# Differential attention with top-2 routed experts on one core: the difference of the one-tile chunk is made by VectorE in every second pair of heads only, by GpSimd in the others

## The chip, the cores and the metric

The kernel runs on one core of one Trainium2 chip. The metric is the device time of one execution in microseconds (us); less is better. The engines are TensorE (PE, with its weight loads as PEld), VectorE (DVE), ScalarE (ACT), GpSimd (POOL) and SyncE (SP, which issues the DMAs of the hardware queue).

## The reference: what is computed

`x` is 8 sequences of 512 tokens of 128 features. One layer of attention with 16 heads of 8 features and two key projections, then a layer of 8 experts of which each token takes 2:

```
s1 = q @ k1.T * SCALE ; s2 = q @ k2.T * SCALE          (causal mask on both)
attn = softmax(s1) - sigmoid(lambda) * softmax(s2)
attn = attn / max(sum(abs(attn)), 1e-6)
x  = layernorm(x + (attn @ v) @ Wo.T)
xn = layernorm(x) * gamma + beta ; p = softmax(xn @ router.T / 1.5)
x  = layernorm(x + sum over the top 2 experts e of p[e] * silu(xn @ W1[e]) @ W2[e])
```

## The kernel before

**Chunks and slots.** One body of the program handles one sequence ("batch") `b`. The attention of a batch is cut into 40 chunks, one for each slot of a body: 8 pairs of heads with 5 chunks each (`SLOTS = PAIRS * KINDS`). A chunk is a row of 512 score columns. The kind of a chunk (`c % 5`) says which query tiles of the pair it holds: kind 0 is one tile of 512 columns (tile 3 of the first head), kind 3 the same of the second head, kind 2 two tiles of 256 columns, kinds 1 and 4 one of 384 and one of 128. Chunks 0, 10, 20, 30 are of kind 0 in the even pairs, chunks 5, 15, 25, 35 of kind 0 in the odd pairs.

**What a chunk goes through.** PE writes both score maps to PSUM (lines 1117, 1119; slot `c`). DVE takes the row maxima (line 989, same slot). ACT makes `exp` with the row sums (line 700, slot `c+1`), into the ring `exps` with 7 places. DVE inverts the second sum (`inv_l2`, line 964, slot `c+2`); POOL makes `lam_l1` from the first (line 614). Then comes the difference `exps2 * coefficient - exps1`, written over the second half of the same ring place (`diff = exps[:, :, 1, :]`, so that the profile names it `exps`). POOL makes it at slot `c+4` with one TENSOR_SCALAR for each tile (line 623) and one TENSOR_TENSOR of 512 columns (line 627). For the kinds in `DVE_KINDS = (0,)` DVE makes it at slot `c+3` in place of POOL: a `coef` of one column (line 974) and one fused SCALAR_TENSOR_TENSOR of 512 columns (line 978). DVE sums the absolute values (line 999, slot `c+5`), PE transposes the difference (line 1151, slot `c+5`), ACT copies it out (line 707), PE multiplies with the values (line 1140).

**Side tasks.** The work of everything else is laid in between by hand, in tables that give each task its slot. Prep tasks (`PREP_SLOTS`) make the projections of batch `b+1`; POOL's part of them is lines 635 and 637, SP's part comes `PARTS_SLOT` slots later. Post tasks belong to batch `b-1` for slots 0 to 39, to `b-2` for 40 to 79, to `b-3` from 80 on: `count` (slot 29) and `place` (31) work out where each token goes; `scatter` (8 indirect DMAs issued by POOL, line 646) writes the tokens to DRAM in the order of the experts; `sorted` (43) loads them back as `xg` (SP, line 498); `turn` (44, 51, 58, 65) transposes four tiles on PE (line 1086); `hidden` and `expert` are the two matmuls of each of 15 tiles (lines 1094 and 1100; DVE's part of `hidden` is `hT`, line 934); `y_out` stores four tiles (SP, line 516); `gather` (8 indirect DMAs on POOL, line 655) fetches them back and `combine` adds them (DVE, line 946). DVE does its part of a task one slot after the table's slot, POOL two slots after, PE, ACT and SP in it. Within a slot every engine runs its queue in the order of the program: chunk work and side tasks have no priority over one another.

**Banks.** The PSUM results of side tasks go in turn to two banks, `side0` and `side1` (`placed_in % banks`, in order of the tasks). A task waits until the reader of the task before it in the same bank is done (line 1034).

**The semaphores of the difference.** `diff_ready(n, c)` gives the semaphore and the count on which ACT (ring place free), DVE (line 996) and PE (line 1148) wait: `diff_dve_done` for a chunk made by DVE, `diff_done` for one made by POOL.

Of the kernel before, what the change touches and what calls it, by code (L numbers as in the profile page):

```python
# [61 lines left out]
EXP_RING, DIFF_RING = 7, 12  # L62


DVE_KINDS = (0,)
PAIR_CHUNKS = (((3, 0, 0),), ((2, 0, 0), (0, 0, 384)), ((1, 0, 0), (1, 1, 256)), ((3, 1, 0),), ((2, 1, 0), (0, 1, 384)))
PLACE_OF_TILE = {3: 0, 2: 1, 0: 2, 1: 3}
PAIRS = NH // 2
KINDS = len(PAIR_CHUNKS)
SLOTS = PAIRS * KINDS  # L70
# [12 lines left out]

SIDE = {}
POST_SLOTS = {"spread": 7, "den_T": 10, "divide": 10, "out_proj": 12, "norms": 17, "xn_T": 21, "logits": 23, "router_exp": 24, "count": 29, "place": 31, "sorted": 43, "norm3": 96, "finish": 98}
HIDDEN_SLOTS = (45, 46, 49, 51, 53, 55, 59, 60, 64, 66, 68, 70, 73, 75, 77)
EXPERT_SLOTS = (48, 50, 52, 54, 56, 58, 62, 63, 67, 69, 71, 73, 76, 77, 79)
WEIGHT_SLOTS = (41, 43, 45, 47, 49, 51, 55, 56, 61, 62, 62, 66, 69, 70, 70)
TURN_SLOTS = (44, 51, 58, 65)
Y_OUT_SLOTS = (57, 67, 77, 83)  # L90
SCATTER_SLOTS = (31, 32, 32, 34, 34, 35, 36, 37)
GATHER_SLOTS = (82, 83, 85, 85, 87, 88, 88, 90)
COMBINE_SLOTS = (86, 86, 88, 90, 91, 91, 91, 93)
STACK_SLOT = 33
WEIGHTS_AHEAD = 4
PARTS_SLOT = 7
PREP_SLOTS = (15, 18, 22, 23, 24)


def units_of(c):  # L100

    pair, kind = divmod(c, KINDS)
    first = pair * 2 * NT
    for t, second, col in PAIR_CHUNKS[kind]:
        yield t, pair, second, col, first + NT * second + PLACE_OF_TILE[t]
# [15 lines left out]

REDUCTIONS = [0]
EXPS = [0]
SCALED = [0]
for _c in range(SLOTS):
    REDUCTIONS.append(REDUCTIONS[-1] + len(reductions(_c)))
    EXPS.append(EXPS[-1] + 2 * len(list(units_of(_c))))
    SCALED.append(SCALED[-1] + (0 if _c % KINDS in DVE_KINDS else len(list(units_of(_c)))))
SETS = PAIRS * len(SUM_SETS)


# [63 lines left out]
def build(nc, x, wqT, wk1T, wk2T, wvT, woT, lam, gamma, beta, rwT, w12, out):  # L195
    ctx = ExitStack()
    with ctx:  # L197
# [8 lines left out]
        def signal(name, per_batch, step=1):  # L206
            signals.append(Signal(ctx.enter_context(nc.semaphore(name)), per_batch, step))
            return signals[-1]
# [118 lines left out]
        inv_l2_done = signal("inv_l2_done", SETS)  # L327
        lam_l1_done = signal("lam_l1_done", SETS)
        scaled_done = signal("scaled_done", SCALED[SLOTS])
        diff_done = signal("diff_done", PAIRS * (KINDS - len(DVE_KINDS)))  # L330
        coef_done = signal("coef_done", PAIRS * len(DVE_KINDS))
        diff_dve_done = signal("diff_dve_done", PAIRS * len(DVE_KINDS))
        abs_done = signal("abs_done", REDUCTIONS[SLOTS])
        trans_done = signal("trans_done", SLOTS)
        diffT_copied = signal("diffT_copied", SLOTS)
# [114 lines left out]

        def diff_ready(n, c):

            pair, kind = divmod(c, KINDS)
            here = kind in DVE_KINDS
            same = [i for i in range(KINDS) if (i in DVE_KINDS) == here]
            made, count = (diff_dve_done if here else diff_done), pair * len(same) + sum(i <= kind for i in same)
            return made.sem, made.after(n, count)

        def earlier(n, c, by):
# [109 lines left out]
        def _(pool):  # L569
# [29 lines left out]
            def body(b, stages):  # L599
                for slot in range(SLOTS):  # L600
                    for n, c in chunks(b, stages, slot, LAG_DIFF):
                        pair, kind = divmod(c, KINDS)
                        ring = ring_e(n, c)
                        count = pair * len(SUM_SETS) + SUM_SET_OF[kind] + 1
                        if kind in (0, 2, 3):
# [7 lines left out]
                                lam_all[:, head_of(pair, kind // 3):head_of(pair, kind // 3) + 1].broadcast_to([P, wide])  # L613
                            nc.gpsimd.tensor_tensor(lam_l1[:, mine], sums[:, 0, mine], lam, ALU.mult)\
                                .then_inc(lam_l1_done.sem, 1)
                        if kind in DVE_KINDS:
                            continue

                        pool.wait_ge(lam_l1_done.sem, lam_l1_done.after(n, count))
# [9 lines left out]
                    for task, n, bank in side_tasks(b, slot, 2 * LAG_SIDE):  # L629
# [9 lines left out]
                        if name == "scatter":  # L639
                            i = task[2]  # L640
# [8 lines left out]
                        if name == "gather":  # L649
                            i = task[2]  # L650
# [116 lines left out]
        def _(dve):  # L767
# [69 lines left out]
            def body(b, stages):  # L837
                for slot in range(SLOTS):
                    route(b, stages, slot, 0)
                    for n, c in chunks(b, stages, slot, LAG_DEN):  # L840
                        if (c + 1) % (SLOTS // 2) == 0:

                            i = (c + 1) // (SLOTS // 2)
# [5 lines left out]
                    for task, n, bank in side_tasks(b, slot, LAG_SIDE):  # L849
# [77 lines left out]
                        if name == "hidden":  # L927
                            j = task[2]
                            i = n * TILES + j
# [7 lines left out]
                        if name == "combine":  # L937
                            i = task[2]
# [25 lines left out]
                            nc.vector.reciprocal(inv_l2[:, mine], sums[:, 1, mine]).then_inc(inv_l2_done.sem, 1)  # L964
                    for n, c in chunks(b, stages, slot, LAG_EXP + 2):
                        pair, kind = divmod(c, KINDS)
                        if kind in DVE_KINDS:

                            (t, _, second, _, i), ring = next(units_of(c)), ring_e(n, c)
                            h = head_of(pair, second)  # L970
                            count = pair * len(DVE_KINDS) + DVE_KINDS.index(kind) + 1
                            dve.wait_ge(exp_done.sem, exp_done.after(n, EXPS[c + 1]))
                            dve.wait_ge(inv_l2_done.sem, inv_l2_done.after(n, pair * len(SUM_SETS) + SUM_SET_OF[kind] + 1))
                            nc.vector.tensor_scalar(coef[:, i:i + 1], sums[:, 0, i:i + 1], lam_all[:, h:h + 1],
                                                    inv_l2[:, i:i + 1], ALU.mult, ALU.mult)\
                                .then_inc(coef_done.sem, 1)
                            dve.wait_ge(coef_done.sem, coef_done.after(n, count))
                            nc.vector.scalar_tensor_tensor(out=diff[:, ring, :], in0=exps[:, ring, 1, :],
                                                           scalar=coef[:, i:i + 1], in1=exps[:, ring, 0, :],
                                                           op0=ALU.mult, op1=ALU.subtract).then_inc(diff_dve_done.sem, 1)  # L980
# [200 lines left out]
```

## Time and profile before

| what | value |
|---|---|
| median of 3 runs | 1152.73 us (1149.02 to 1153.8) |
| the profiled execution | 1139.17 us, span 1137.3 us |
| DVE busy | 935.6 us, 82% of the span |
| PE busy / PEld busy | 908.5 us, 80% / 726.7 us, 64% |
| POOL busy | 846.0 us, 74% |
| ACT busy | 841.1 us, 74% |
| mean granted clock of PE | 0.877 |

The shares are means over the whole span. The span has a start of some 60 us, in which the first batch has no neighbours, seven bodies in which attention and side tasks run together, and an end from about 1017 us on, in which only side tasks of the last batch are left. The execution that was profiled was 13.6 us faster than the median of the runs beside it, so durations are set against its own 1139.17 us.

### The profile page before, as it was taken

What the parts mean: (1) busy time and instruction counts of PE and PEld (TensorE: products, weight loads), DVE (VectorE), ACT (ScalarE), POOL (GpSimd) and SP (SyncE); (2) the same over time, 40 slices, a digit from 0 to 9 for tenths busy, and PEclk for the clock granted to TensorE, in tenths of its full rate; (3) what the DMA queues carried; (4) which work ended last, traced back from release to release, by engine and by line L of the source; (5) the groups of instructions that cost most, each with busy time, mean ns of one, the idle gap of its engine ahead of it and who ended that gap; (6) DMA issues with size and microseconds to landing.
All of it is one profiled execution on the core that took longest, in us unless ns stands there. A gap on an engine that the chain in (4) does not pass through costs nothing. (4 is left out here: it accounts for less than half of the span.)

```text
span 1137.3 us, 27887 instructions
## 1 busy us (share of the span) xinstructions
PE 908.5 (80%) x8522; PEld 726.7 (64%) x8522; DVE 935.6 (82%) x2425; ACT 841.1 (74%) x2706; POOL 846.0 (74%) x1144
## 2 busy tenths in 40 slices
PE   2487877879889788978889778978889888978681
PEld 1255555657678576766677566767677676768571
DVE  0499998889998899899999899889999899955132
ACT  1499988688887788788888788787888778853130
POOL 3389978788778888698778988798878986781503
PEclk9579788778998899889999899889999799988696
DMA  3703400533246623482237523582237523246562
GB/s 100 177 10 98 108 1 16 140 100 117 84 122 176 182 76 108 132 246 88 75 122 186 174 74 108 156 238 71 77 120 198 154 73 113 87 147 198 172 215 61
DMA packets 117045, 139.38 MB, mean 123 GB/s; under 512 B 11042, under 2 KB 99490, under 8 KB 116898
## 3 DMA queue, kind: packets, MB, share of 16 engines
q1 hardware_dynamic: 112802, 129.21, 38.3%
q0 software_dynamic: 4096, 8.40, 2.6%
q8 instruction: 69, 1.13, 0.4%
q14 instruction: 78, 0.64, 0.2%
HBM read 107.81 MB, written 29.75 MB: 121 GB/s over the span
## 5 line engine op out<-in xcount | busy, mean ns | idle before, releaser
L700 ACT ACTIVATE exps<-scores,neg_max 128x512 f32<-128x512 f32 (+3 forms) x1024 | 542.9, 551 | 102.1 <-DVE neg_max L989 101.1
L989 DVE TENSOR_REDUCE neg_max<-scores 128x1 f32<-128x512 f32 (+3 forms) x896 | 423.4, 524 | 51.3 <-PE scores L1119 49.1
L627 POOL TENSOR_TENSOR exps<-exps 128x512 f32<-128x512 f32 x256 | 326.7, 1276 | 21.4
L623 POOL TENSOR_SCALAR exps<-exps,inv_l,lam_l 128x384 f32<-128x384 f32 (+3 forms) x448 | 272.7, 615 | 87.2 <-DVE inv_l L964 75.6
L1151 PE MATMUL trans<-ident,exps 128*128 128x128 f32 x1280 | 234.6, 313 | 91.3 <-ACT diffT L707 69.3
L1117 PE MATMUL scores<-stack 72*128 72x512 bf16 (+3 forms) x1024 | 272.6, 335 | 16.6 <-DMA stack<-parts_dram 15.6
L1151 PEld LDWEIGHTS trans<-ident,exps 128*128 128x128 f32 x1280 | 158.4, 158 | 155.3 <-issue 95.3
L700 ACT ACTIVATION_READ_ACCUMULATOR exps<-scores,neg_max 128x1 f32 x1024 | 235.8, 230 | 0.0
L999 DVE TENSOR_REDUCE abs_sum<-exps 128x1 f32<-128x512 f32 (+3 forms) x448 | 222.8, 520 | 8.8 <-POOL exps L627 8.8
L707 ACT ACTIVATE diffT<-trans 128x512 f32<-128x512 f32 x320 | 196.4, 614 | 35.1 <-PE trans L1151 34.3
L1119 PE MATMUL scores<-causal_bf,ident_bf 128*128 128x128 bf16 x1024 | 209.0, 237 | 0.0
L1117 PEld LDWEIGHTS scores<-stack 72*128 72x128 bf16 x1024 | 110.6, 108 | 68.5 <-DMA stack<-parts_dram 15.8
L1094 PE MATMUL side<-xgT,w_sb 128*128 128x128 f32 x792 | 121.3, 301 | 1.9 <-DMA w_sb<-w_dram 1.0
L1100 PE MATMUL side<-w_sb,hT 128*128 128x128 f32 x824 | 114.6, 283 | 6.4 <-DVE hT L934 6.4
L1119 PEld LDWEIGHTS scores<-causal_bf,ident_bf 128*128 128x128 bf16 x1024 | 111.2, 109 | 6.9
L1094 PEld LDWEIGHTS side<-xgT,w_sb 128*128 128x128 f32 x792 | 107.5, 211 | 11.8 <-issue 4.8
L1100 PEld LDWEIGHTS side<-w_sb,hT 128*128 128x128 f32 x824 | 102.2, 195 | 10.6 <-DVE hT L934 6.7
L1140 PE MATMUL heads<-diffT,v_sb 128*32 128x128 f32 x2560 | 106.8, 287 | 0.0
L646 POOL DMA_INDIRECT x_sorted_dram<-xh,place_int x64 | 66.8, 1043 | 44.7 <-DVE owner_int L925 29.9
L655 POOL DMA_INDIRECT y_back<-y_sorted_dram,place_int x64 | 63.7, 995 | 46.0 <-issue 44.4
L1140 PEld LDWEIGHTS heads<-diffT,v_sb 128*32 128x32 f32 x2560 | 62.2, 112 | 29.1 <-issue 16.6
L753 ACT ACTIVATE tanh_sb<-side 128x512 f32<-128x512 f32 x99 | 60.6, 613 | 25.8 <-PE side L1094 25.1
(138 smaller groups left out, 921.6 us busy)
## 6 DMA issues: line engine op xcount, KB each, us to landing
w_sb<-w_dram SPq DMA_DIRECT2D x120, 512.0 KB, 3.8
stack<-parts_dram SPq DMA_DIRECT2D x288, 96.0 KB
parts_dram<-parts SPq DMA_DIRECT2D x104, 128.0 KB
xg<-x_sorted_dram SPq DMA_DIRECT2D x24, 256.0 KB, 4.2
y_sorted_dram<-y_sorted SPq DMA_DIRECT2D x24, 256.0 KB, 4.5
x_in<-x_dram SPq DMA_DIRECT2D x8, 256.0 KB, 4.7
x_res<-x_dram SPq DMA_DIRECT2D x8, 256.0 KB, 4.8
o_dram<-y_out SPq DMA_DIRECT2D x8, 256.0 KB, 2.3
```

Source lines behind the costliest of these rows:

```text
L623: nc.gpsimd.tensor_scalar(diff[:, ring, col:col + w], exps[:, ring, 1, col:col + w], inv_l2[:, i:i + 1], lam_l1[:, i:i + 1], ALU.mult, ALU ...
L627: nc.gpsimd.tensor_tensor(diff[:, ring, :], diff[:, ring, :], exps[:, ring, 0, :], ALU.subtract)\
L700: nc.scalar.activation(exps[:, ring, k, col:col + w], scores[:, c % 2, k, col:col + w], ACT.Exp, bias=neg_max[:, c % 2, k, i:i + 1], accum ...
L707: nc.scalar.activation(diffT[:, ring_d(n, c), :], trans[:, :], ACT.Copy)\
L989: nc.vector.tensor_reduce(neg_max[:, c % 2, k, i:i + many], scores[:, c % 2, k, col:col + many * w].rearrange("p (i w) -> p i w", w=w), AX ...
L999: nc.vector.tensor_reduce(abs_sum[:, place:place + (many - 1) * step + 1:step], diff[:, ring_e(n, c), col:col + many * w].rearrange("p (i ...
L1094: last = nc.tensor.matmul(bank[:, f * P:(f + 1) * P], w12_sb[:, w, f * P:(f + 1) * P], xgT[:, j // NT % 2, j % NT, :], start=True, stop=True)
L1100: last = nc.tensor.matmul(bank[:, 0:D], hT[:, (n * TILES + j) % 2, f, :], w12_sb[:, (n * TILES + j) % WEIGHTS_AHEAD, F + f * D:F + (f + 1) ...
L1117: nc.tensor.matmul(scores[:, c % 2, k, col:col + w], stack[:, 0, h, t * P:(t + 1) * P], stack[:, 1 + k, h, 0:w], start=True, stop=False)
L1119: last = nc.tensor.matmul(scores[:, c % 2, k, col + w - P:col + w], ident_bf[:, :], causal_bf[:, :], start=False, stop=True)
L1140: last = nc.tensor.matmul(heads[k * STRIP:(k + 1) * STRIP, t * P:(t + 1) * P], v_sb[:, i, NG * k + g, :], diffT[:, ring_d(n, source), col: ...
L1151: last = nc.tensor.transpose(trans[:, i * P:(i + 1) * P], diff[:, ring_e(n, c), i * P:(i + 1) * P], ident[:, :])
```

## The change

`DVE_KINDS` goes. In its place `DVE_CHUNKS` lists the chunks whose difference DVE makes: 5, 15, 25 and 35, one in each odd pair. The difference of chunks 0, 10, 20 and 30 is made by POOL, as those of the kinds 1 to 4 are. The counts of the semaphores follow. Beside it the tables of the side tasks differ: `hidden` and `expert` of tiles 9 to 14 come two slots later (of the 15 `hidden` tasks the last now has slot 79, of the `expert` tasks 81), the weights of tiles 2 to 14 one to three slots later, one `y_out`, one `scatter` a slot later, one projection a slot earlier, and SP's store of the parts a slot earlier.

```diff
-DVE_KINDS = (0,)
...
-HIDDEN_SLOTS = (45, 46, 49, 51, 53, 55, 59, 60, 64, 66, 68, 70, 73, 75, 77)
-EXPERT_SLOTS = (48, 50, 52, 54, 56, 58, 62, 63, 67, 69, 71, 73, 76, 77, 79)
+HIDDEN_SLOTS = (45, 46, 49, 51, 53, 55, 59, 60, 64, 68, 70, 72, 75, 77, 79)
+EXPERT_SLOTS = (48, 50, 52, 54, 56, 58, 62, 63, 67, 71, 73, 75, 78, 79, 81)
...
-SCATTER_SLOTS = (31, 32, 32, 34, 34, 35, 36, 37)
+SCATTER_SLOTS = (31, 32, 33, 34, 34, 35, 36, 37)
...
+DVE_CHUNKS = [c for c in range(SLOTS) if c % (2 * KINDS) == KINDS]
 SCALED = [0]
 for _c in range(SLOTS):
...
-    SCALED.append(SCALED[-1] + (0 if _c % KINDS in DVE_KINDS else len(list(units_of(_c)))))
+    SCALED.append(SCALED[-1] + (0 if _c in DVE_CHUNKS else len(list(units_of(_c)))))
...
-            pair, kind = divmod(c, KINDS)
-            here = kind in DVE_KINDS
-            same = [i for i in range(KINDS) if (i in DVE_KINDS) == here]
-            made, count = (diff_dve_done if here else diff_done), pair * len(same) + sum(i <= kind for i in same)
+            by_dve = sum(i <= c for i in DVE_CHUNKS)
+            made, count = (diff_dve_done, by_dve) if c in DVE_CHUNKS else (diff_done, c + 1 - by_dve)
             return made.sem, made.after(n, count)
...
-                        if kind in DVE_KINDS:
+                        if c in DVE_CHUNKS:
                             continue
...
-                        if kind in DVE_KINDS:
+                        if c in DVE_CHUNKS:
...
-                            count = pair * len(DVE_KINDS) + DVE_KINDS.index(kind) + 1
+                            count = DVE_CHUNKS.index(c) + 1
```

POOL's queue at slots 33 to 35, from the first scatter of a batch on, before (line 646 is the scatter, 614 `lam_l1`, 623 and 627 the difference):

```order
L646 DMA x_sorted_dram<-xh,place_int 1920x128
L614 TENSOR_TENSOR lam_l<-sums,lam_all 128x3
L646 DMA x_sorted_dram<-xh,place_int 1920x128 x2
L623 TENSOR_SCALAR exps<-exps,inv_l,lam_l 128x384
L623 TENSOR_SCALAR exps<-exps,inv_l,lam_l 128x128
L627 TENSOR_TENSOR exps<-exps 128x512
```

And after (the program is two lines shorter above this place, so 644 is the scatter, 612 `lam_l1`, 621 and 625 the difference):

```order
L644 DMA x_sorted_dram<-xh,place_int 1920x128
L612 TENSOR_TENSOR lam_l<-sums,lam_all 128x3
L621 TENSOR_SCALAR exps<-exps,inv_l,lam_l 128x512
L625 TENSOR_TENSOR exps<-exps 128x512
L644 DMA x_sorted_dram<-xh,place_int 1920x128
L621 TENSOR_SCALAR exps<-exps,inv_l,lam_l 128x384
L621 TENSOR_SCALAR exps<-exps,inv_l,lam_l 128x128
L625 TENSOR_TENSOR exps<-exps 128x512
L644 DMA x_sorted_dram<-xh,place_int 1920x128
```

The two instructions of chunk 30 stand between the first scatter and the second, and the third scatter stands behind chunk 31.

PE's queue at slots 28 and 29 of a batch in the middle, around `count`, before (line 1094 is `hidden`, 1100 `expert`, 1069 `count`; the matmuls of the scores are left out):

```order
L1094 MATMUL side0<-xgT,w12_sb 128x128 x4
L1140 MATMUL heads<-diffT,v_sb 32x128 x4
L1151 MATMUL trans<-ident,exps 128x128 x4
...
L1100 MATMUL side1<-w12_sb,hT 128x128 x4
L1069 MATMUL side0<-ones,hit 8x1 x4
```

And after (1092 is `hidden`, 1098 `expert`, 1067 `count`), from slot 27 on:

```order
L1098 MATMUL side0<-w12_sb,hT 128x128 x4
L1138 MATMUL heads<-diffT,v_sb 32x128 x8
L1149 MATMUL trans<-ident,exps 128x128 x4
...
L1092 MATMUL side1<-xgT,w12_sb 128x128 x4
L1138 MATMUL heads<-diffT,v_sb 32x128 x4
L1149 MATMUL trans<-ident,exps 128x128 x4
...
L1067 MATMUL side0<-ones,hit 8x1 x4
```

Before, `count` writes the bank of the `hidden` task of the slot ahead of it, which DVE reads; after, it writes the bank of an `expert` task two slots back, which ACT reads.

## Rows read from the trace of the kernel before

**Rows 1.** Windows: length; busy PE, PEld, DVE, ACT, POOL; clock; DMA. Two batches.

```profile
62.50:158.50 96.00, 76.92 (x754) 53.75 (x754) 92.36 (x224) 89.38 (x302) 85.36 (x119) 0.86 0.23 62
...
526.60:652.40 125.80, 105.95 (x1065) 85.48 (x1065) 118.26 (x303) 104.09 (x339) 105.56 (x140) 0.95 0.45 136
```

**Rows 2.** Waits from 183.1 to 906.7 us: us in total, times, longest.

```profile
DVE neg_max L989 <- PE scores L1119: 30.0, 29, 4.4
...
DVE abs_sum L999 <- POOL exps L627: 1.3, 4, 0.4
...
POOL exps L623 <- DVE inv_l L964: 55.9, 46, 2.4
```

**Rows 3.** Windows of three stretches: first batch, slots 13 to 32, 33 to 44.

```profile
79.00:137.00 58.00, 47.08 (x455) 32.60 (x452) 55.65 (x133) 55.73 (x188) 54.74 (x76) 0.88 0.34 90
541.00:602.00 61.00, 52.94 (x538) 43.01 (x536) 57.58 (x159) 49.51 (x159) 47.87 (x66) 0.97 0.30 97
602.00:639.00 37.00, 31.32 (x302) 24.00 (x300) 33.13 (x79) 32.01 (x107) 32.89 (x43) 0.86 0.87 248
```

**Rows 4.** Timeline of DVE, slot 13: start us, us, what.

```profile
541.30 0.14 DVE L964 RECIPROCAL inv_l<-sums 128x3 f32<-128x3 f32 x1
541.55 0.27 DVE L974 TENSOR_SCALAR coef<-sums,lam_all,inv_l 128x1 f32<-128x1 f32 x1
...
542.53 1.28 DVE L989 TENSOR_REDUCE neg_max<-scores 128x1 f32<-128x512 f32 x2
```

**Rows 5.** DVE's fused difference: all 64 (ns min/median/max), and one at slot 3.

```profile
L978 DVE SCALAR_TENSOR_TENSOR exps<-exps,coef x64: 750/958/1817, 48.9 to 995.9; 128x512 f32<-128x512 f32 x64
...
503.99 1.70 DVE L978 SCALAR_TENSOR_TENSOR exps<-exps,coef 128x512 f32<-128x512 f32 x1
```

**Rows 6.** Groups by form, DVE: busy, mean ns | idle before.

```profile
L934 DVE SCALAR_TENSOR_TENSOR hT<-tanh_sb,side 128x512 f32<-128x512 f32 x99 | 67.0, 677 | 11.5 <-ACT tanh_sb L753 11.3
```

**Rows 7.** Timeline of POOL around the scatters of one batch.

```profile
470.59 0.77 POOL L623 TENSOR_SCALAR exps<-exps,inv_l,lam_l 128x512 f32<-128x512 f32 x1 [2.44 <-DVE inv_l L964]
471.44 1.27 POOL L627 TENSOR_TENSOR exps<-exps 128x512 f32<-128x512 f32 x1
...
476.85 1.11 POOL L646 DMA_INDIRECT x_sorted_dram<-xh,place_int  x1 [1.72 <-DVE owner_int L925]
...
496.60 0.98 POOL L646 DMA_INDIRECT x_sorted_dram<-xh,place_int  x1 [0.17 <-issue]
...
505.12 1.52 POOL L623 TENSOR_SCALAR exps<-exps,inv_l,lam_l 128x384 f32<-128x384 f32 x2
...
509.43 1.09 POOL L623 TENSOR_SCALAR exps<-exps,inv_l,lam_l 128x384 f32<-128x384 f32 x2
...
517.20 0.77 POOL L623 TENSOR_SCALAR exps<-exps,inv_l,lam_l 128x512 f32<-128x512 f32 x1 [1.24 <-DVE inv_l L964]
```

**Rows 8.** Timelines of SP, PE and DVE, the chain from the scatters on.

```profile
500.48 0.44 SPq L516 DMA_DIRECT2D y_sorted_dram<-y_sorted  x1
501.34 4.35 SPq L498 DMA_DIRECT2D xg<-x_sorted_dram  x4
...
509.56 1.09 PE L1086 MATMUL side<-ident,xg 128*128 128x128 f32 x4 [1.97 <-DMA xg<-x_sorted_dram]
...
513.35 1.29 DVE L989 TENSOR_REDUCE neg_max<-scores 128x1 f32<-128x512 f32 x2 [3.22 <-PE scores L1119]
...
532.03 0.60 PE L1086 MATMUL side<-ident,xg 128*128 128x128 f32 x4
```

**Rows 9.** PE at `count`, DVE at `place`, and windows with PE's granted clock.

```profile
464.70 0.35 PE L1069 MATMUL side<-ones,hit 128*8 128x1 f32 x8 [2.22 <-DVE hT L934]
...
474.95 0.22 DVE L906 TENSOR_TENSOR place_of<-hit,side 128x64 f32<-128x64 f32 x1 [2.31 <-PE side L1080]
...
464.30:474.30 10.00, 9.60 (x65) 8.55 (x65) 7.61 (x20) 6.15 (x21) 6.09 (x9) 0.66 0.22 64
...
504.30:514.30 10.00, 7.84 (x47) 5.26 (x46) 6.75 (x14) 6.31 (x20) 9.35 (x13) 0.50 0.85 267
```

More of the change, by code:

```diff
@@ L85 @@
 POST_SLOTS = {"spread": 7, "den_T": 10, "divide": 10, "out_proj": 12, "norms": 17, "xn_T": 21, "logits": 23, "router_exp": 24, "count": 29, "place": 31, "sorted": 43, "norm3": 96, "finish": 98}
-HIDDEN_SLOTS = (45, 46, 49, 51, 53, 55, 59, 60, 64, 66, 68, 70, 73, 75, 77)
-EXPERT_SLOTS = (48, 50, 52, 54, 56, 58, 62, 63, 67, 69, 71, 73, 76, 77, 79)
-WEIGHT_SLOTS = (41, 43, 45, 47, 49, 51, 55, 56, 61, 62, 62, 66, 69, 70, 70)
+HIDDEN_SLOTS = (45, 46, 49, 51, 53, 55, 59, 60, 64, 68, 70, 72, 75, 77, 79)
+EXPERT_SLOTS = (48, 50, 52, 54, 56, 58, 62, 63, 67, 71, 73, 75, 78, 79, 81)
+WEIGHT_SLOTS = (41, 43, 46, 48, 50, 52, 56, 57, 62, 65, 65, 69, 72, 73, 73)
 TURN_SLOTS = (44, 51, 58, 65)
-Y_OUT_SLOTS = (57, 67, 77, 83)
-SCATTER_SLOTS = (31, 32, 32, 34, 34, 35, 36, 37)
+Y_OUT_SLOTS = (57, 68, 77, 83)
+SCATTER_SLOTS = (31, 32, 33, 34, 34, 35, 36, 37)
 GATHER_SLOTS = (82, 83, 85, 85, 87, 88, 88, 90)
@@ L95 @@
 WEIGHTS_AHEAD = 4
-PARTS_SLOT = 7
-PREP_SLOTS = (15, 18, 22, 23, 24)
+PARTS_SLOT = 6
+PREP_SLOTS = (15, 18, 21, 23, 24)
 def units_of(c):
@@ L329, in build @@
         scaled_done = signal("scaled_done", SCALED[SLOTS])
-        diff_done = signal("diff_done", PAIRS * (KINDS - len(DVE_KINDS)))
-        coef_done = signal("coef_done", PAIRS * len(DVE_KINDS))
-        diff_dve_done = signal("diff_dve_done", PAIRS * len(DVE_KINDS))
+        diff_done = signal("diff_done", SLOTS - len(DVE_CHUNKS))
+        coef_done = signal("coef_done", len(DVE_CHUNKS))
+        diff_dve_done = signal("diff_dve_done", len(DVE_CHUNKS))
         abs_done = signal("abs_done", REDUCTIONS[SLOTS])
```

## The prediction

> **What bounds the kernel now.** I read the windows first, one batch at a time, because the shares of the whole span mix stages. A batch with experts takes 125.8 us; DVE is busy for 118.3 of them and POOL for 105.6 [rows 1]. Then I read the waits of the six middle batches: in 724 us DVE waits 30.0 us for scores and only 1.3 us for POOL, while POOL waits 55.9 us for DVE's reciprocal [rows 2]. So DVE is mostly the engine that sets the pace, and POOL follows with slack. But the slack isn't spread evenly. In slots 13 to 32 DVE is busy for 57.6 of 61.0 us and POOL for 47.9; in slots 33 to 44 it is 33.1 and 32.9 of 37.0 [rows 3]. The timeline of POOL shows why. Its last wait is 1.72 us in front of the first scatter, at 476.85; from there it works without a wait for data until 517.20, where it waits 1.24 us [rows 7]. Inside that run lies a chain that everything follows: last scatter at 496.60, SP's load of `xg` at 501.34, PE's transposes at 509.56 after 1.97 us of waiting for that load, and DVE's next maxima at 513.35 after 3.22 us without work [rows 7, 8]. The reader is to see two regimes in each body: a long one that DVE sets (A, from slot 5 to `place`) and a short one that POOL's queue sets (B, from `place` to slot 44).
>
> **What the change costs and saves.** Durations come from the profiled execution, so the sum starts at its 1139.17 us; the median of the runs shown is 1152.73, 1.2% above, and I scale the result by that.
>
> One chunk taken from DVE: with the pair, the reciprocal starts at 541.30, `coef` at 541.55, and the next maxima start at 542.53 [rows 4]. Without it the maxima would follow the reciprocal's 0.14 us at about 541.4. That is 1.1 us. The dearest case is at slot 3, where the fused operation alone took 1.70 us in place of 0.75 [rows 5], so about 2 us. Four chunks a batch, 32 in all.
>
> One chunk given to POOL: TENSOR_SCALAR of 512 columns 0.77 us, TENSOR_TENSOR 1.27 us, and the 0.08 us between them [rows 7]: 2.1 us, 67 us in all. It is nearly twice what DVE is spared, so the change pays only where POOL's part falls on idle time.
>
> The Trainium skill (GPSIMD Engine Reference, Key points and Engine selection) says that GpSimd is about half as fast as VectorE on a two-input operation, and that it contends with VectorE instructions that read two SBUF tensors. The first speaks against this change and the rows agree (1.27 us for POOL's half of the work). By the second, taking away 32 such DVE instructions would also speed POOL up: its two TENSOR_SCALARs took 1.52 us beside a DVE pair and 1.09 us without one [rows 7], which would be 32 x 0.43 = 13.8 us of POOL's time back. The rows bear that out only for chunk 0, since at slot 13 the pair ran at its floor [rows 4, 5]; I leave it out of the sum.
>
> *Regime A.* Chunks 10 and 20 leave DVE: 2 x 1.1. In the six bodies that carry expert work, one `hT` of 0.68 us [rows 6] also moves from before `place` to behind it (DVE runs `hidden` one slot late: 12 tasks up to slot 72 before, 11 after). POOL gets 4.2 us more in a stretch where it is idle for 13 of 61 us [rows 3], which hides it; uncovered it would cost 4.2 us a body. A gives 7 x 2.2 + 6 x 0.7 = 19.6 us back.
>
> *Regime B.* Chunk 30 goes into POOL's queue between the first and the second scatter. Behind it wait seven scatters, and for them SP's `xg` load, PE's `turn` and all of DVE behind that. DVE is spared chunks 30 and 0 here and gets the moved `hT`, but it was not the one waited for. Each of seven bodies pays 2.1 us: 14.7 us. Chunk 0 comes behind the last scatter, in front of the first gather; the 1.24 us wait at 517.20 and the next ones absorb it, so I count nothing. If that cover is gone it is 2.1 us a body.
>
> *First batch.* From 79 to 137 us there are no experts, DVE is busy for 55.7 and POOL for 54.7 of 58.0 us [rows 3]. Two chunks (20 and 30) add 4.2 us to POOL; it can give back at most 58.0 - 54.7 = 3.3 us of gaps. So it costs 1 to 4 us; I take 4, as those gaps are between instructions.
>
> *The bank of `count`.* PE stood still 2.22 us in front of `count`, waiting for DVE's read of a `hidden` result [rows 9]. In the new order the bank was last an `expert` result that ACT has read. Behind that stall PE's granted clock is 0.66 in the mean of 464.3 to 474.3, so at 1.2 GHz for part of it, and DVE then waits 2.31 us for `place` [rows 9]. A PE that is not stalled may stay at 2.4 GHz and finish `place` sooner. The bound is 0 on one side and POOL's own wait of 1.72 us there on the other [rows 7]; I take 1.0 us in each of six bodies: 6 us gained.
>
> *Clock at slot 44.* From 504.3 to 514.3 the clock was 0.50 [rows 9], and the first `turn` took 1.09 us where the next took 0.60 [rows 8]. PE had no side matmuls in slots 40 to 43; now it has one `hidden` at 39 and the last `expert` at 41. Three such groups lie on the chain (transposes, values, transposes), some 1.4 us. Between nothing and all of it I take 0.7 in five bodies: 3.5 us gained.
>
> *The end.* Tile 9's `hidden` now comes behind tile 8's `expert`, one place where PE no longer has work while it waits: 1 us lost. Weights, `y_out` and the prep slots move by about as much as the work that uses them, and no engine waits long for them: 0.
>
> Sum: 1139.2 - 19.6 + 14.7 + 4 - 6 - 3.5 + 1 = 1129.8 us; times 1152.73 / 1139.17 that is **1143 us**.
>
> **The rivals.**
>
> 1. *The trade cancels.* The clock falls as before in both places. Then the sum is 1139.2 - 19.6 + 14.7 + 4 + 1 = 1139.3, or 1153 us. For it: POOL sets more of the time from `place` to slot 44 now, and PE waits on POOL there. Against it: the stall at `count` is really gone.
> 2. *GpSimd's queue stays behind (the slower side).* Chunk 0 in front of the gathers isn't absorbed: POOL goes from 476.85 to 517.20 with 4.2 us more and only 1.24 us of waiting to give, then has the gathers. If it is still late when PE wants the next difference, each of seven bodies pays 2.1 us more and the clock gains nothing: 1139.3 + 14.7 = 1154.0, or 1168 us. It decides once POOL has no wait left between `place` and slot 14. Against it: PE and DVE stand 1.97 and 3.22 us for `xg` in just that stretch [rows 8], in which POOL catches up.
> 3. *DVE is the bound everywhere and POOL's queue is elastic.* All 32 chunks at 1.1 us, the `hT` moves change nothing: 35 us less, 1104, or 1117 us. For it: DVE's 118.3 of 125.8 us. Against it: the chain over the scatters, in which the added work stands in line.
> 4. *The last tile comes too late.* `expert` 14 moves to slot 81 and its store, which waits for it, stays at 83, in front of `xg` on SP's queue. Before, that store was issued at 500.48 and `xg` at 501.34 [rows 8]; about one slot of 3.1 us (125.8 / 40) is the price if it slips past the scatters' end: 6 x 3.1 on the cancelled sum, 1158, or 1172 us. Against it: the scatters now end 2.1 us later too.
>
> **How the numbers follow.** Chances: forecast 0.42 (own range 1136 to 1150), rival 1 0.27, rival 2 0.16, rival 3 0.07, rival 4 0.08. The range of 8 in 10 has to reach into rivals 2 and 3, since both signs hold much of the chance: 1128 to 1164. A measurement of this kernel can tell about 0.5% from no change: below 1147 is faster, above 1158.5 slower. Faster: 0.33 of the forecast, 0.05 of rival 1, all of rival 3, so 0.45. Slower: 0.14 of rival 2, 0.05 of rival 4, 0.05 of rival 1 and 0.01 of the forecast, 0.25. Within: 0.30.
>
> **What would show it.** In the profile after: DVE's line 978 (by its new number) 32 times, POOL's TENSOR_SCALAR of 512 columns 96 times; DVE busy about 900 us, POOL about 911. POOL's wait for the reciprocal falls from 55.9 to some 25 us in the six middle batches. From the first to the last scatter 21.9 us in place of 19.8. No wait of PE for `hT` in front of `count`, and a shorter wait of DVE in front of `place`. The first batch some 100 us in place of 96.0. The prediction is wrong if POOL's queue isn't what `xg` waits for, if `place` isn't sooner with the stall gone, or if the waits of DVE on POOL's differences (1.3 us) grow to tens of us.

## The result: 3.3% slower, and the profile after

| | before | after |
|---|---|---|
| median | 1150.88 us (1148.64 to 1153.8) | **1187.51 us** (1184.9 to 1191.45) |
| ratio | | 1.0331, 95% interval 1.0295 to 1.0366 |

The forecast was 1143 us, faster; the time is 37 us slower and outside the range. The profiled execution of the changed kernel took 1184.9 us (span 1183.1); that of the kernel before was itself 12 us under its median, so the two traces set side by side overstate the difference by some 9 us (45.7 against 36.6). Later runs went to chips of different speed (the kernel before took 1153.26 us on the chip of `e1` to `e4` and 1136.5 on those of the others), so each is given as a ratio to the kernel before on its own chip. Traces of `e3` and `e0` are from different chips. Line numbers of the kernels with the other split are 2 lower than those of before.

The page of the changed kernel, the busy times and the groups that answer to [rows 2, 5, 6] (busy, mean ns | idle before, by whom):

```profile
PE 919.1 (78%) x8522; PEld 731.2 (62%) x8522; DVE 924.7 (78%) x2361; ACT 841.4 (71%) x2706; POOL 900.3 (76%) x1208
...
L625 POOL TENSOR_TENSOR exps<-exps 128x512 f32<-128x512 f32 x288 | 367.1, 1275 | 24.0
...
L1149 PEld LDWEIGHTS trans<-ident,exps 128*128 128x128 f32 x1280 | 157.2, 156 | 185.9 <-POOL exps L625 93.9
L997 DVE TENSOR_REDUCE abs_sum<-exps 128x1 f32<-128x512 f32 (+3 forms) x448 | 223.7, 522 | 24.6 <-POOL exps L625 24.4
```

POOL rose by 54 us and DVE fell by only 11. No engine is busier than 78%: the kernel lost time by waiting. Whole windows, the first batch and two bodies (columns as in [rows 1]):

```profile
61.70:159.30 97.60, 76.25 (x756) 53.04 (x754) 89.95 (x217) 88.67 (x302) 91.79 (x128) 0.87 0.26 61
401.30:534.80 133.50, 108.29 (x1065) 86.86 (x1065) 118.78 (x295) 104.69 (x339) 114.76 (x151) 0.94 0.44 129
534.80:663.60 128.80, 112.13 (x1065) 90.77 (x1065) 115.31 (x295) 104.42 (x339) 109.13 (x145) 0.89 0.46 132
```

The first batch took 97.6 us where it had taken 96.0, and the bodies 119 to 134 where the one of [rows 1] took 125.8. The last copy of the last chunk comes 29 us later than in the trace of before, and the stretch behind it, in which only side tasks are left, is 17 us longer (141 us for 124). Little can be read from that last part: its program is the same in `e0` and `e3`, and it took 124 us in one and 136 in the other. Who waited, from slot 8 of the second batch to slot 8 of the eighth (184 to 928.7 us; total, times, longest):

```profile
DVE neg_max L987 <- PE scores L1117: 38.6, 43, 5.2
DVE abs_sum L997 <- POOL exps L625: 13.9, 20, 2.1
...
DVE rest L855 <- ACT parts L717: 9.1, 6, 1.8
...
PE trans L1149 <- POOL exps L625: 36.9, 29, 2.8
...
PE side L1067 <- DVE hit L829: 11.9, 6, 2.1
...
POOL exps L621 <- DVE inv_l L962: 44.3, 37, 2.5
```

DVE now waits 13.9 us for POOL where it waited 1.3 [rows 2], and PE waits 36.9 us for POOL's differences where it waited 13.1 (21.0 in `e0`, another execution of the same kernel). But POOL itself still waits 44.3 us for DVE: each is late for the other at different places, and neither is simply the bound.

### The profile page after: what moved, and what is told of

Read it like the earlier page. It is cut to its first block and busy times, and to the rows that moved or that the text cites. A ratio compares the mean times of both kernels' runs of the same rounds, so it can differ in the third digit from the quotient of the medians.

```text
span 1183.1 us, 27887 instructions
## 1 busy us (share of the span) xinstructions
PE 919.1 (78%) x8522; PEld 731.2 (62%) x8522; DVE 924.7 (78%) x2361; ACT 841.4 (71%) x2706; POOL 900.3 (76%) x1208
## 5 line engine op out<-in xcount | busy, mean ns | idle before, releaser
L625 POOL TENSOR_TENSOR exps<-exps 128x512 f32<-128x512 f32 x288 | 367.1, 1275 | 24.0
L621 POOL TENSOR_SCALAR exps<-exps,inv_l,lam_l 128x384 f32<-128x384 f32 (+3 forms) x480 | 292.5, 615 | 72.2 <-DVE inv_l L962 55.9
L997 DVE TENSOR_REDUCE abs_sum<-exps 128x1 f32<-128x512 f32 (+3 forms) x448 | 223.7, 522 | 24.6 <-POOL exps L625 24.4
L1098 PE MATMUL side<-w_sb,hT 128*128 128x128 f32 x808 | 116.6, 290 | 11.1 <-DVE hT L932 10.9
L1138 PE MATMUL heads<-diffT,v_sb 128*32 128x128 f32 x2560 | 110.6, 288 | 3.9 <-issue 3.8
L644 POOL DMA_INDIRECT x_sorted_dram<-xh,place_int x64 | 67.3, 1052 | 42.4 <-DVE owner_int L923 31.4
L932 DVE SCALAR_TENSOR_TENSOR hT<-tanh_sb,side 128x512 f32<-128x512 f32 x100 | 67.6, 676 | 26.2 <-ACT tanh_sb L751 24.9
```

What stands on the lines that cost most here:

```text
L621: nc.gpsimd.tensor_scalar(diff[:, ring, col:col + w], exps[:, ring, 1, col:col + w], inv_l2[:, i:i + 1], lam_l1[:, i:i + 1], ALU.mult, ALU ...
L625: nc.gpsimd.tensor_tensor(diff[:, ring, :], diff[:, ring, :], exps[:, ring, 0, :], ALU.subtract)\
L997: nc.vector.tensor_reduce(abs_sum[:, place:place + (many - 1) * step + 1:step], diff[:, ring_e(n, c), col:col + many * w].rearrange("p (i ...
L1098: last = nc.tensor.matmul(bank[:, 0:D], hT[:, (n * TILES + j) % 2, f, :], w12_sb[:, (n * TILES + j) % WEIGHTS_AHEAD, F + f * D:F + (f + 1) ...
L1138: last = nc.tensor.matmul(heads[k * STRIP:(k + 1) * STRIP, t * P:(t + 1) * P], v_sb[:, i, NG * k + g, :], diffT[:, ring_d(n, source), col: ...
```

## The experiments

**Which part costs: the split or the tables?** The change holds two things. Each was run alone, and then the parts of each. `e1` is the changed kernel with all tables of before; `e2` the kernel before with all new tables.

> Only the split of the difference is changed (GpSimd makes chunks 0, 10, 20, 30); every table of side tasks is that of before. Theory Q (GpSimd's queue): the seven bodies of the changed kernel are 22.6 us longer because GpSimd has 2.1 us more per chunk where it has no slack, and the 23.2 us after the last of them come from the tables; this kernel then takes about 1151 + 22 = 1173 us. Theory T (tables): all of the loss comes from the later expert tasks; this kernel then takes 1151 us or a little less.

> Only the tables are changed; VectorE makes the difference of every chunk of kind 0, as before. Theory Q: 1151 + 23 = 1174 us, nearly all of the difference after 928 us. Theory T: 1187 us.

Measured 1172.76 us, 1.0198 (1.0150 to 1.0246), for the split and 1172.20 us, 1.0191 (1.0138 to 1.0243), for the tables. Two almost equal losses, whose product 1.039 is near the 1.033 of both. So the tables don't serve the split, and the half that the forecast counted as nothing or a small gain lost as much as the other.

**The split, chunk by chunk.** The tables of before, and only this line in `e3` and `e4` (and `e10` below):

```diff
-DVE_CHUNKS = [c for c in range(SLOTS) if c % (2 * KINDS) == KINDS]
+DVE_CHUNKS = [c for c in range(SLOTS) if c % KINDS == 0 and c not in (10, 20)]    # e3
+DVE_CHUNKS = [c for c in range(SLOTS) if c % KINDS == 0 and c != 30]              # e4
+DVE_CHUNKS = [c for c in range(SLOTS) if c % KINDS == 0 and c != 25]              # e10
```

> Tables of before; GpSimd makes only chunks 10 and 20, in the stretch that the prediction called regime A. As the prediction had it, each of seven bodies gains 2.2 us and the first batch loses some 3: 1151 - 12 = 1139 us. Theory Q in its strict form (GpSimd has no usable slack anywhere): half of the loss of the kernel with all four chunks, 1162 us.

> Tables of before; GpSimd makes only chunk 30, whose two instructions stand in front of the scatters. As the prediction had it, seven bodies lose 2.1 us each and the first batch some 2: 1151 + 15 = 1166 us. If the scatters are not what the rest waits for: 1151 us.

Measured 1162.38 us, 1.0080 (1.0051 to 1.0110), and 1158.42 us, 1.0048 (1.0019 to 1.0076). Chunks 10 and 20, on which the forecast's gain rested, lose 9 us. Chunk 30 costs 5.5 us where 14.7 was counted. What is left of the 1.98% is 0.7% for chunk 0 (some 8 us), which was counted as absorbed. No run has chunk 0 alone; the intervals of the three ratios put it anywhere from 1 to 15 us, if the chunks' costs add.

**Relief and load apart.** `e0` is the kernel before once more. In `e5` DVE's fused difference of chunks 0, 10, 20 and 30 covers 1 of 512 columns (the other columns keep the second map's exponentials as ACT wrote them, so the output leaves part of the work out). In `e6` DVE does all it did, and POOL makes the same two instructions on a spare buffer beside it.

```diff
+                            wide = 1 if c % (2 * KINDS) == 0 else WIDE            # e5
...
+                        if c % (2 * KINDS) == 0:                                  # e6
...
+                            nc.gpsimd.tensor_scalar(spare[:, 0, :], spare[:, 1, :], ...)
...
+                            nc.gpsimd.tensor_tensor(spare[:, 0, :], spare[:, 0, :], spare[:, 1, :], ALU.subtract)
```

> The kernel before, unchanged, for a second trace: its profiled execution of 1139 us was 1% below the median of its runs, so the traces so far may overstate what every other kernel loses. Expected: a ratio of 1.00 and a profiled execution near 1150 us.

> Kernel before, but VectorE's fused difference of chunks 0, 10, 20 and 30 covers one column in place of 512 (the other 511 columns of that difference are left out, so those chunks carry wrong values). It shows what VectorE's relief is worth if GpSimd gets nothing: some 0.7 to 1.6 us for each of 32 chunks. Theory D (VectorE sets the pace in most places, as the prediction had it): 25 us less, 1128 us. Theory Q (GpSimd's queue sets the pace in as many places): 10 us less or fewer, 1141 to 1151 us.

> Kernel before, but GpSimd also runs the two instructions that it would need for chunks 0, 10, 20 and 30, at the same place in its queue, on a spare buffer that nobody reads; VectorE still makes those differences. It shows what the load is worth alone. Theory D: only the four chunks of the first batch and chunk 30 of the others cost, some 20 us, 1172 us. Theory Q: 30 us or more, 1181 us and up, since the split alone lost 20 us net of VectorE's relief. If the loss came from the difference being ready later, and not from the load: under 10 us.

Measured 1137.47 us for `e0` (1.0007, 0.9979 to 1.0035), 1127.09 us for `e5` (0.9904, 0.9877 to 0.9931) and 1179.91 us for `e6` (1.0376, 1.0340 to 1.0413). In `e5` the group of fused differences falls from 65.0 to 46.4 us, since a narrow one still has its fixed part, and 11 us of those 18.6 arrive (by the ratio; 9 by the medians): 0.6 of what DVE is spared. Load alone costs 43 us, 1.34 us of the 2.1 us that each chunk takes. At these rates the whole split would be 32 x (1.34 - 0.6 x 1.1) = 22 us slower, an estimate that `e1` bears out (0.0198 x 1153 = 23 us). The waits of DVE from 183 to 906 us, in `e0` and in `e5`, hint at where the rest of the relief went:

```profile
DVE neg_max L989 <- PE scores L1119: 22.5, 22, 3.5
```

```profile
DVE neg_max L990 <- PE scores L1120: 30.6, 28, 3.4
...
DVE rest L857 <- ACT parts L719: 3.8, 5, 0.8
```

DVE, relieved, waits 8 us longer for scores and 3.8 us for ACT where it waited 1.1. The first of these is no proof by itself, since another trace of the kernel before has 30.0 us there [rows 2]; the time is what shows that part of the relief is lost. That it was busy for 118 of 125.8 us [rows 1] didn't make it the bound.

**Why does load cost so much?** The timelines of DVE and then POOL at slots 17 to 19 of one body, first in `e0` (start us, us):

```profile
553.53 1.10 DVE L788 TENSOR_SCALAR x_twice<-r,mv,rstd 128x128 f32<-128x128 f32 x4
554.55 1.12 DVE L788 TENSOR_SCALAR xh<-r,mv,rstd 128x128 f32<-128x128 f32 x4
...
558.84 1.10 DVE L788 TENSOR_SCALAR y_out<-acc,mv,rstd 128x128 f32<-128x128 f32 x4
...
553.81 1.11 POOL L672 TENSOR_TENSOR rstd<-var_eps,minus_half 128x4 f32<-128x4 f32 x1
554.82 0.26 POOL L614 TENSOR_TENSOR lam_l<-sums,lam_all 128x3 f32<-128x3 f32 x1
555.93 1.52 POOL L623 TENSOR_SCALAR exps<-exps,inv_l,lam_l 128x384 f32<-128x384 f32 x2 [0.85 <-DVE inv_l L964]
```

and in `e3`, where chunk 10 has pushed POOL's queue back:

```profile
558.30 1.25 DVE L786 TENSOR_SCALAR x_twice<-r,mv,rstd 128x128 f32<-128x128 f32 x4
559.47 2.07 DVE L786 TENSOR_SCALAR xh<-r,mv,rstd 128x128 f32<-128x128 f32 x4
...
564.51 1.75 DVE L786 TENSOR_SCALAR y_out<-acc,mv,rstd 128x128 f32<-128x128 f32 x4
...
559.28 1.40 POOL L625 TENSOR_TENSOR exps<-exps 128x512 f32<-128x512 f32 x1
560.77 0.30 POOL L667 TENSOR_SCALAR var_eps<-mv 128x4 f32<-128x4 f32 x1
561.16 1.04 POOL L670 TENSOR_TENSOR rstd<-var_eps,minus_half 128x4 f32<-128x4 f32 x1
...
564.14 1.27 POOL L625 TENSOR_TENSOR exps<-exps 128x512 f32<-128x512 f32 x1
```

The reader is to see the same four instructions on `xh` taking 2.07 us in place of 1.12, and those on `y_out` 1.75 in place of 1.10, exactly while POOL has a 512-column TENSOR_TENSOR running. POOL used to be between its big instructions there. The groups by form add it up, for `e0`, for `e3`, and for the changed kernel:

```profile
L788 DVE TENSOR_SCALAR x_twice<-r,mv,rstd 128x128 f32<-128x128 f32 x32 | 9.8, 370 | 0.0
L788 DVE TENSOR_SCALAR xh<-r,mv,rstd 128x128 f32<-128x128 f32 x32 | 8.9, 343 | 0.0
```

```profile
L786 DVE TENSOR_SCALAR xh<-r,mv,rstd 128x128 f32<-128x128 f32 x32 | 14.8, 524 | 0.0
...
L786 DVE TENSOR_SCALAR x_twice<-r,mv,rstd 128x128 f32<-128x128 f32 x32 | 10.8, 401 | 0.0
```

```profile
L786 DVE TENSOR_SCALAR xh<-r,mv,rstd 128x128 f32<-128x128 f32 x32 | 14.8, 524 | 0.0
L786 DVE TENSOR_SCALAR x_twice<-r,mv,rstd 128x128 f32<-128x128 f32 x32 | 13.3, 476 | 0.0
L786 DVE TENSOR_SCALAR y_out<-acc,mv,rstd 128x128 f32<-128x128 f32 x32 | 12.1, 440 | 3.1 <-POOL rstd L670 3.1
```

With `y_out` (8.8 us in `e0`, 12.1 in `e3`), the line takes 27.5 us in `e0`, 37.7 in `e3` and 40.2 in the changed kernel. The single instructions of `e3` say which of POOL's hold them up. Of the 96, 13 start while a 512-column TENSOR_TENSOR of POOL runs (one in `e0`), and they take 1.29 us in the median where the others take 0.34: that is all of the 10 us. The first on `xh` runs from 559.47 to 560.76, and POOL's instruction ends at 560.68. The 23 that start beside POOL's TENSOR_SCALARs of 384 or 128 columns take 0.34 us, as those beside none do. The Trainium skill (SBUF — State Buffer, Who interferes with whom) says that a TENSOR_SCALAR or copy of VectorE in a two-port mode and an instruction of GpSimd exclude each other, the later one waiting for the whole of the other. The trace agrees beside POOL's TENSOR_TENSORs, 1.12 against 2.07 us for the same four, and not beside its TENSOR_SCALARs, so here the measurement narrows the rule.

It isn't the whole price of load either. In `e6`, where the load is pure, all groups of DVE together grow by 20 us and the kernel loses 43. For the rest the traces show POOL being late: PE waits 38.0 us for POOL's differences there, for 21.0 in `e0`.

Two other causes were tried against that one. `e11` is `e3` with POOL's `proj` task (`parts`, lines 635 and 637 of before) ahead of the chunk's difference in its slot: in `e3` DVE's `rest` waits 12.8 us for those parts, a wait that `e0` doesn't have. `e10` gives POOL another chunk, 25, alone.

> Tables of before; GpSimd makes the difference of chunk 25 alone (8 times) in place of VectorE. GpSimd's work per batch grows by 2.1 us at slot 29, between the parts of the projections and the scatters. Theory Q (GpSimd's added work costs about 1.4 us of each 2.1 wherever it stands, VectorE's relief gives 0.35 us a chunk): 8 us more, ratio 1.007. Theory W (the loss of chunks 10 and 20 is the wait of rest for parts in slots 24 and 25 and that of chunk 30 is the scatters' queue; elsewhere GpSimd has room): ratio 0.996 to 1.000.

> Chunks 10 and 20 on GpSimd with the tables of before (1.008 of before), but GpSimd makes the parts of the projections ahead of a slot's difference in place of behind it. Theory W (the loss is the new wait of VectorE's rest for GpSimd's parts, 2.1 us in five bodies): 10 us come back, ratio 0.998 to 1.001, and that wait is gone. Theory Q (GpSimd's load costs whatever the order): ratio 1.006 to 1.009.

`e11` took 1147.98 us, 1.0102 (1.0070 to 1.0134): nothing came back. But its wait of `rest` only fell from 12.8 to 9.7 us, so it shows that the order in the slot is no cure, not that the wait is free. `e10` took 1131.00 us, 6.5 us less than the kernel before, **0.9942** (0.9919 to 0.9965): the same 2.1 us of POOL's work, at slot 29, makes the kernel 0.6% faster. So load need not cost. In `e10` the three normalise groups stay at 9.4, 8.9 and 8.9 us. Another small group of DVE's, `hit<-hit` of 32 columns, grows from 3.8 to 7.8 us there, and the kernel is faster all the same: some us of slower DVE instructions need not cost either.

Then the contention was to be taken away. `e14` and `e15` are the kernel before and `e3` with `normalise` on 4 of 128 columns; `e16` and `e17` the same two with one MEMSET in its place. All four leave out the layer norms, so what the router sees differs; each pair differs only in chunks 10 and 20.

```diff
-                    last = nc.vector.tensor_scalar(dst[:, t, :], src[:, t, :], ...)
+                    last = nc.vector.tensor_scalar(dst[:, t, 0:4], src[:, t, 0:4], ...)    # e14, e15
+                return nc.vector.memset(dst[:, 0, 0:4], 0.5)                               # e16, e17
```

> The kernel before, but VectorE's normalise (x_twice, xh, y_out: 96 TENSOR_SCALARs of 128x128) makes 4 columns of 128 only; the rest of the tiles stays zero, so the routing has other data. It is the base for the next run. VectorE is spared 2 us a body in slots 17 to 19: ratio 0.985 to 0.998.

> Chunks 10 and 20 on GpSimd with the tables of before (1.008 of before), and VectorE's normalise narrowed to 4 columns as in the run before this one, against which it is read. Theory C (contention: with chunk 10 on GpSimd, GpSimd is busy while VectorE normalises, and those TENSOR_SCALARs take up to 2.07 us for four in place of 1.12, 11 us in all): with almost no such work left, the two chunks no longer cost anything: this run is 0.995 to 1.002 of the run before it. Theory Q (GpSimd's load costs by itself): this run stays 1.006 or more above it.

> The kernel before, with VectorE's normalise (12 TENSOR_SCALARs a batch) replaced by one MEMSET of 4 columns for each tile; the layer norms' outputs are constants, so the routing has other data. It is the base for the next run. VectorE is spared up to 3 us a body in slots 14 to 19: ratio 0.975 to 0.992 of before.

> Chunks 10 and 20 on GpSimd with the tables of before and the same MEMSETs in place of normalise; read against the run before it. With the normalise narrowed to 4 columns the split still cost 0.65% (1139.30 against 1131.93), and the trace shows that the narrow instructions were held up just as the wide ones, 9.7 us in all (each waits out an instruction of GpSimd), so that run did not take the contention away. Theory C (VectorE's TENSOR_SCALARs are what loses: 11 us): with none left, this run is 0.993 to 1.001 of the run before it. Rival (GpSimd's load of chunks 10 and 20 delays its later differences, whatever VectorE runs): it stays at 1.006 or more.

| chunks 10, 20 on POOL | with DVE's normalise | 4 columns | none |
|---|---|---|---|
| DVE makes them | 1 | 1131.93 us | 1120.14 us |
| POOL makes them | 1.0080 | 1139.30 us | 1123.72 us |
| cost | 0.80% | 0.65% | 0.32% |

The first column is `e3`. The runs of `e16` lie from 1118.08 to 1123.97 us and those of `e17` from 1119.91 to 1125.18, so the last cost can hardly be told from none. By the spread of the runs the three costs are good to about 0.3% each, so that the first two are alike and the third is lower by 0.5%, give or take 0.4; as ratios to the kernel before the four are 0.9955, 1.0028, 0.9845 and 0.9866.

The narrow version missed its aim: in `e15` the four narrow instructions on `xh` still took 1.86 us beside POOL (0.90 in `e14`), so what they wait out doesn't depend on their own size. With none left, about 0.5 of the 0.8% is gone. Two things limit that test. It spares DVE some 25 us of work besides (the narrow version only 6), and a DVE with more room may hide POOL's lateness whatever the contention; no run separates the two. And not all contention is gone: DVE's `hit<-probs,top` takes 5.0 us in `e17` for 1.3 in `e16`, as it takes 5.1 in `e3` for 1.3 in `e0`. Body by body, `e17` runs 0.5 us a body shorter than `e16` in the five middle ones, and the copies of the chunks at slots 19 and 20 no longer fall back by the 1.5 us a body that they do in `e3` and `e15`, which is the best sign for the contention. `e17` is longer in the first batch (2.8 us), the second (2.1) and the last (3.2), and 2.8 us shorter behind its last copy.

**The tables.** `e7` is the kernel before with the new `HIDDEN_SLOTS`, `EXPERT_SLOTS`, `WEIGHT_SLOTS` and `Y_OUT_SLOTS` only.

> Kernel before with only the tables of hidden, expert, weights and y_out of the changed kernel; scatter, parts and prep slots as before. If the later expert tasks are what the tables cost: 1172 us, as with all tables. If it is the scatter, parts or prep slots: 1151 us.

Measured 1154.17 us, 1.0141 (1.0078 to 1.0204): most of the tables' 1.9%. PE's waits from 183 to 906 us, in `e0` and in `e7`:

```profile
PE side L1086 <- DMA xg<-x_sorted_dram: 6.6, 5, 2.2
```

```profile
PE side L1086 <- DMA xg<-x_sorted_dram: 25.5, 5, 6.4
```

That looks like rival 4, the late last tile. Two kernels tested it, with the last store at slot 84, behind `xg` on SP's queue: `e8` on `e7`, `e9` on the kernel before.

```diff
-Y_OUT_SLOTS = (57, 68, 77, 83)
+Y_OUT_SLOTS = (57, 68, 77, 84)
```

> Expert tables of the change on the kernel before (as in the run of the expert tables alone, 1.014 of before), but the last store of y_out moved from slot 83 to 84, so that SP issues xg in front of it. Theory R (the last tile is late and holds its store, and xg stands behind the store on SP's queue): most of the 1.4% comes back, ratio 1.000 to 1.003, and PE's first turn starts some 6.3 us behind the issue of xg in place of 7.9 to 9.6. Rival (the later experts cost their time on PE, DVE and ACT themselves, whatever stands on SP's queue): ratio stays at 1.011 or more.

> The kernel before, with only the last store of y_out at slot 84 in place of 83. In the kernel before, xg was followed by the first turn after 6.0 to 6.4 us where no store was in front of it and after 7.1 to 8.4 us where there was one. Theory R: some 1.5 us less in each of five or six bodies, ratio 0.992 to 0.995. Rival (the store's place is hidden, or the gathers, which wait for that store, now start late): ratio 1.000 or above.

`e8` took 1161.88 us, 1.0208 (1.0168 to 1.0248), and `e9` 1143.97 us, 1.0063 (1.0040 to 1.0086). Both are slower, not faster, so the forecast of that theory failed. But the two runs don't clear the late tile. The first gather waits for that last store (the kernel's own semaphores say so), so a later store holds POOL's queue. POOL's wait in front of the gathers from 183 to 906 us, in `e0` and in `e9`:

```profile
POOL y_back L655 <- issue: 6.6, 34, 0.3
```

```profile
POOL y_back L655 <- issue: 20.5, 28, 4.8
```

It is 14.7 us in `e7` and 31.4 in `e8`, whose wait of PE for `xg` is only down to 20.4. The move exchanged one wait for another, and what the late tile costs in `e7` stays open. The next theory came from SP's queue. In the middle bodies of the kernels up to there the first `turn` came 28 to 34 us after the first load of `stack`, and in `e7` those loads stand behind a weight load that waits for `expert` 10. The first loads of `stack` and that of `xg` in `e0`, then `e7`, then `e12`, in the same body:

```profile
604.07 12.04 SPq L535 DMA_DIRECT2D stack<-parts_dram  x27
...
627.34 2.66 SPq L498 DMA_DIRECT2D xg<-x_sorted_dram  x4
```

```profile
611.62 11.77 SPq L535 DMA_DIRECT2D stack<-parts_dram  x27
...
634.87 5.70 SPq L498 DMA_DIRECT2D xg<-x_sorted_dram  x4
```

```profile
587.06 3.67 SPq L535 DMA_DIRECT2D stack<-parts_dram  x9
...
603.11 3.67 SPq L535 DMA_DIRECT2D stack<-parts_dram  x9
...
632.28 4.58 SPq L498 DMA_DIRECT2D xg<-x_sorted_dram  x4
```

`e12` (on `e7`) and `e13` (on the kernel before) put the stack first: `PARTS_SLOT = 6`, `STACK_SLOT = 30`, and the weight loads that wait for experts 9 and 10 in another order (`e12`: the load of tile 13 at slot 71 in place of 73; `e13`: that of tile 14 at 71 in place of 70).

> Expert tables of the change alone (1.014 of before), but with SP's queue in another order: three of the four groups of stack loads at slots 30 to 32 in place of 33 to 35, PARTS_SLOT 6, and the load of the weights of tile 13 at slot 71 in place of 73, so that no weight load that waits for expert 10 stands in front of the stack. Theory S (SP's queue: in every kernel so far the first turn comes 29 to 33 us after the first stack load of its body, the DMA engines are over 0.9 busy in between, and the later experts hold the load of the weights of tile 14, behind which the stack loads stand): all of the 1.4% comes back, ratio 0.995 to 1.001. Rival (the later experts cost their time on the engines): ratio 1.012 or more.

> The kernel before with only SP's queue in another order: PARTS_SLOT 6, STACK_SLOT 30, and the load of the weights of tile 14 at slot 71 in place of 70. In the kernel before that load waits for expert 10 in front of the last stores of parts, and the stack loads wait for those to land (5 us). Theory S: the stack loads start some 5 to 9 us sooner in the body, the loads of xg find the DMA engines free, and the time falls by 1 to 3 us a body: ratio 0.980 to 0.993. Rival (xg waits for the scatters, which start no sooner): ratio 0.998 to 1.002, with the first turn as far behind the last scatter as before.

`e12` took 1153.96 us, 1.0145 (1.0114 to 1.0177); `e13` 1137.52 us, 1.0010 (0.9985 to 1.0035). The first group of the stack's loads starts 24.6 us sooner than in `e7` (587.06 against 611.62) and the second 8.5 us sooner, PE's wait for `xg` falls from 25.5 to 15.4 us, and the median doesn't move. This theory fell too. The fixed distance was two things that move together, not a cause: in `e12` it is 51 to 56 us.

The single traces leave a doubt, which is not settled here. Against `e0`, the last copy of the last chunk comes 17.7 us later in `e7`, but 12.0 in `e8` and 8.2 in `e12`; the stretch behind it is 0.9, 7.0 and 5.4 us longer. So in its bodies each of the two may have won something, which the medians don't show.

A third candidate is PE's clock at `count` and `place`, where the windows of [rows 9] were read. From the copy of chunk 24 to that of chunk 28 in two bodies each, in `e0` and in `e7` (length, PE busy, granted clock, DMA):

```profile
466.60:479.40 12.80, 12.70 (x109) 0.90 0.37 113
593.30:606.40 13.10, 13.00 (x119) 0.91 0.38 118
```

```profile
469.10:483.90 14.80, 13.74 (x96) 0.77 0.16 50
...
728.70:746.90 18.20, 17.50 (x100) 0.56 0.13 41
```

Over five bodies the stretch takes 66.6 us in `e0` and 76.8 in `e7`, with clocks down to 0.56, that is mostly at 1.2 GHz, where `e0` has 0.88 to 0.91 in four bodies and 0.73 in one. But the first trace of the same kernel, before, has 72.5 us there with clocks of 0.67 to 0.89, `e8` has 68.4 with 0.92 to 0.94 in four of five and is slower than `e7`, and `e13`, as fast as before, has 72.6. So the clock moves the stretch, and doesn't account for the time.

## Why the prediction was wrong

**Regime A, "19.6 us back": wrong sign.** The steps "one chunk taken from DVE is 1.1 us" and "POOL gets 4.2 us more in a stretch where it is idle for 13 of 61 us, which hides it" both failed. Only some 0.6 of the relief arrives (`e5`), since DVE's neighbours are nearly as late as DVE. And POOL's idle time wasn't free: it was the time in which DVE's normalise ran undisturbed. Chunks 10 and 20 cost 9 us (`e3`), and some 5 of them, give or take 4, are gone where normalise is left out (`e17` against `e16`). That DVE was held up is shown; that this is what costs is the likeliest reading and not shown to the end.

**The rule was read in one direction.** The forecast weighed that taking fused operations from DVE would speed POOL up, and left it out. The rows carried the other half, POOL's work slowing DVE down, and no term priced it: DVE's busy time was to fall to about 900 us and fell to 924.7, though the fused operations and their `coef` take 38.6 us for 81.8 before. Of these 43 us, 13 came back in normalise (27.1 to 40.2 us) and some 13 more in other groups together.

**Regime B, "14.7 us" for chunk 30: right mechanism, wrong size.** From the first to the last scatter it takes 22.0 to 24.5 us where it took 19.8, at least the 21.9 foretold, but `e4` costs only 5.5 us in all. Two things were left out of the 2.1 us a body. In the kernel before, `xg` is issued 4.7 to 6.5 us behind the last scatter in the bodies (496.60 and 501.34 in [rows 7, 8]); in `e4` it is 4.3 to 5.3, so that some 0.8 us a body is absorbed in front of `xg`. And DVE's relief was given nothing here; at the rate of `e5` it is 8 x 0.6 x 1.1 = 5 us. With both, 14.7 us becomes some 4, an estimate next to the 5.5.

**Chunk 0, "I count nothing": wrong as far as known.** About 8 us by subtraction (1 to 15), half of the price that rival 2 gave it. DVE's waits for POOL did grow, from 1.3 to 13.9 us, which the text named as a sign of being wrong; but `e4` alone has 10.3, so most of that belongs to chunk 30.

**The bank of `count`, "6 us gained": wrong.** PE's wait for `hT` there is gone, but a wait of 11.9 us for DVE's `hit` stands in the same place (11.1 us for `hT` before): behind the read of the bank DVE was late with the next thing as well. The clock at slot 44, "3.5 us": the first `turn` took 1.09 us as before in all middle bodies but one, so no gain.

**The tables, "0" and "+1": wrong, and the cause is open.** They cost 1.9%, of which the later experts are 1.4 (0.8 to 2.0). Moving the stack's loads ahead gave nothing back in the median. The late last tile is not cleared, since the runs that moved its store made POOL wait for it. Argued only: PE's clock around `place`. Not tried: moving the `hidden` and `expert` tasks one at a time.

**Rivals.** Rivals 2 and 4 were given 1168 and 1172 us and 0.24 between them, each as the only mishap. Both halves did go wrong at about that size, and added; no case had them together, which is why even the range's upper end was low. That the sizes are near is no proof of the two mechanisms: chunk 0 is only a third of the split's loss, and the late tile is open.

## What to carry to other kernels

Before moving an instruction to an engine with idle time, look at what the other engines run in that idle time, DVE's TENSOR_SCALARs and copies above all; the same 2.1 us moved from DVE to POOL cost 0.6 us a time at slots 14 and 24, 0.7 at 34 and (by subtraction) 1.0 at 4, and gained 0.8 at 29, and only runs of single chunks told which. Price relief and load by themselves (a narrowed instruction; the same work on a spare buffer) before adding them up. And when a change comes with retuned tables, time them alone: here they lost as much as the idea.

## What the runs showed of the hardware that was not expected

- DVE's 128x128 TENSOR_SCALARs were held up by POOL's 512-column TENSOR_TENSORs (1.29 us in the median for 0.34, 13 instructions in `e3`) and not by POOL's TENSOR_SCALARs of 384 or 128 columns (0.34 us, 23 instructions).
- TENSOR_SCALARs of 4 columns were held up by POOL as those of 128 columns were: four on `xh` took 1.86 us for 0.90 narrow, 2.07 for 1.12 wide.
- POOL got a little back where DVE's fused operations went: its 448 TENSOR_SCALARs of line 623 took 272.7 us before, and the 480 after took 292.5, though the 32 new ones of 512 columns at 0.77 us [rows 7] are 24.6 us. That gives some 5 us back, a third of the 13.8 that the forecast had worked out and left out.
- A stretch of constant length is no proof of a chain: from the first stack load to the first `turn` it was 28 to 34 us in the kernels up to `e11`, and in `e12` the first loads came 24.6 us sooner than in `e7` without a gain in the median.
